# Adapter table rows stored unsplit, and split by GpSimd when a tile's rows are placed

## The reference, cut to what matters

```
x = x + x W^T + 2 * experts(x)        # W 1024x1024; 8 experts of rank 16, gated by the top 2
x = x + weights[cond] mixed over the 64 rows of a sample
x = x + (x B2[id]^T) A2[id]^T         # 64 adapters of rank 16, one for each sample
x = x + x W3^T + b3 + 2 * (x A3[m]) B3[m]   # 32 adapters of rank 16, one for each sample
```

## Time and profile before

| | us |
|---|---|
| median of three runs | 886.78 |
| span of the profiled execution | 884.5 |
| what lies around the span (median less span) | 2.3 |
| PE busy | 876.8 (99%) |
| DVE busy | 651.4 (74%) |
| ACT busy | 350.5 (40%) |
| POOL busy | 241.3 (27%) |
| granted PE clock, all 40 slices | 9 tenths or more |

### The profile page before, as it was taken

The page is one execution under the profiler, slowest core; times in us unless marked ns, Lnnn a source line. Parts: engine busy times, 40 slices in busy tenths (PEclk is TensorE's granted clock), DMA queues, the critical chain, the costliest instruction groups (busy, mean ns, idle before and its releaser), DMA issues.

```text
span 884.5 us, 15284 instructions
## 1 busy us (share of the span) xinstructions
PE 876.8 (99%) x4668; PEld 810.8 (92%) x4668; DVE 651.4 (74%) x1865; ACT 350.5 (40%) x800; POOL 241.3 (27%) x379
## 2 busy tenths in 40 slices
PE   8999999999999999999999999999999999999997
PEld 7888888888888889999999999999999999999997
DVE  6555444444358634798998899898899899899896
ACT  5544333333334423434434434434334344345333
POOL 1100010010000004415415425325325335235230
PEclk9999999999999999999999999999999999999999
DMA  7978686899663575566666667667667667566674
GB/s 243 311 265 282 207 262 211 284 350 274 191 193 126 162 222 174 164 179 200 213 185 216 202 182 230 196 188 222 192 188 230 185 195 224 186 195 215 196 205 144
DMA packets 105606, 187.71 MB, mean 212 GB/s; under 512 B 20022, under 2 KB 66870, under 8 KB 105526
## 3 DMA queue, kind: packets, MB, share of 16 engines
q1 hardware_dynamic: 105526, 186.76, 68.3%
HBM read 143.20 MB, written 49.81 MB: 218 GB/s over the span
## 4 chain that ended last, share of the span: by engine, by line
PE 96%; DMA 1%; DVE 1%; POOL 1%; SPq 0%; issue 0%; ACT 0%; DVEq 0%; POOLq 0%
PE ps_o L1487 28%; PE ps_w L1521 16%; PE ps_d L1513 15%; PE ps_d L1521 12%; PE ps_s L1487 9%; PE ps_o L1534 5%; PE ps_d L1528 4%; PE ps_o L1556 3%; PE ps_s L1562 1%; PE ps_w L1528 1%; DMA chunk_a_raw<-mov 1%; DMA stat_raw<-x 1%; PE ps_s L1568 0%; PE ps_o L1589 0%; DVE outb L1333 0%
## 5 line engine op out<-in xcount | busy, mean ns | idle before, releaser
L1094 DVE TENSOR_TENSOR stat_lo<-stat_raw,stat_hi 128x1024 fp32r<-128x1024 f32 (+1 forms) x127 | 152.2, 1199 | 22.2 <-ACT stat_hi L798 19.8
L798 ACT ACTIVATE stat_hi<-stat_raw 128x1024 fp32r<-128x1024 f32 (+1 forms) x127 | 116.7, 931 | 12.1 <-POOL stat_raw L682 5.4
L1513 PE MATMUL ps_d<-w_hi,stat_hi 128*128 128x392 f32 x256 | 86.9, 340 | 0.3 <-POOL w_lo L707 0.3
L1513 PE MATMUL ps_d<-w_hi,stat_lo 128*128 128x392 f32 x256 | 86.8, 339 | 0.0
L1513 PE MATMUL ps_d<-w_lo,stat_hi 128*128 128x392 f32 x256 | 86.8, 339 | 0.0
L1487 PE MATMUL ps_o<-chunk_a_hi,stat_hi 128*128 128x512 f32 x216 | 84.3, 390 | 0.9 <-DVE chunk_a_lo L1094 0.9
L1487 PE MATMUL ps_o<-chunk_a_lo,stat_hi 128*128 128x512 f32 x216 | 84.1, 389 | 0.0
L1487 PE MATMUL ps_o<-chunk_a_hi,stat_lo 128*128 128x512 f32 x216 | 84.0, 389 | 0.0
L707 POOL CAST w_hi<-mdraw 128x512 fp32r<-128x512 f32 x32 | 31.3, 977 | 157.0 <-DMA mdraw<-t 156.9
L682 POOL TENSOR_TENSOR stat_raw<-stat_raw,ident 128x128 f32<-128x128 f32 x40 | 20.5, 514 | 186.5 <-DMA stat_raw<-stat 186.5
L1487 PE MATMUL ps_o<-chunk_b_hi,stat_hi 128*128 128x512 f32 x152 | 59.1, 389 | 0.0
(11 more groups left out here) (230 smaller groups left out, 2346.4 us busy)
## 6 DMA issues: line engine op xcount, KB each, us to landing
up<-tu SPq DMA_DIRECT2D x124, 256.0 KB, 4.6
stat_raw<-stat SPq DMA_DIRECT2D x59, 512.0 KB, 4.2
mdraw<-t SPq DMA_DIRECT2D x128, 208.0 KB, 3.2
stat_raw<-x SPq DMA_DIRECT2D x32, 512.0 KB, 3.4
out<-outb SPq DMA_DIRECT2D x30, 512.0 KB, 5.5
t<-md_a SPq DMA_DIRECT2D x16, 576.0 KB, 5.4
rows_raw<-x SPq DMA_DIRECT2D x32, 256.0 KB, 3.7
chunk_a_raw<-mov SPq DMA_DIRECT2D x24, 256.0 KB, 5.5
```

The source lines that it names most:

```text
L798: return nc.scalar.activation(dst, src, ACT.Copy)
L1094: return nc.vector.tensor_tensor(out=dst, in0=src, in1=rounded.bitcast(F32), op=ALU.subtract)
L1513: last = nc.tensor.matmul(plain_bank(t)[:, 0:WCOLS], rows[a][:, k, :], w[c][:, k, :], start=k == 0 and m == 0, stop=k == KB - 1 and m == l ...
```

## The change

The tables hold the products in float32, one value for each instead of two parts. ACT's evacuation of the 27 groups of `D_CHUNKS` writes float32 (the same number of operations, of the same size), DVE's for these groups is gone, and PE, SP and the counts of `dve_ev` follow from that. A stored row is 144 + 128 = 272 columns instead of 416. Each of the three chunks has a buffer of its own. `place_w` and `place_b` now make the rounded part with a `tensor_copy` from float32 to float32r, wait for it, and make the rest with a `tensor_tensor` subtraction that reads `mdraw` and the part just written. `pool_md` and `pool_mb` count two for each tile. `mdraw` shrinks by 2304 bytes in each partition, and everything allocated behind it moves down by that.

```diff
-    RAW_AT, FULL = 2 * ROW, 2 * ROW + KB * RANK
+    RAW_AT, FULL = ROW, ROW + KB * RANK
...
+    def split_out(g):
+        return sum(GROUPS[n][0] in M3_CHUNKS for n in range(g + 1))
...
-            md_a = stages.enter_context(nc.sbuf_tensor("md_a", [P, PER, 2 * ROW], F32R))
-            md_b = stages.enter_context(nc.sbuf_tensor("md_b", [P, PER, 2 * ROW], F32R))
-        mdst = [md_a, md_b, md_a]
+            mdst = [stages.enter_context(nc.sbuf_tensor(f"md_{c}", [P, PER, ROW], F32)) for c in D_CHUNKS]
...
-        mdraw = sb("mdraw", [P, 2 * BT, FULL], F32R)
+        with nc.sbuf_tensor("up3_last", [P, D], F32R) as up3_b:
+            pass
+        mdraw = sb("mdraw", [P, 2 * BT, FULL])
...
             def store_md(c, n):
                 if n == 0:
-                    sp.wait_ge(dve_ev, LAST[c] + 1)
+                    sp.wait_ge(act_ev, LAST[c] + 1)
...
             def load_md(t):
                 if not at(t, 0):
-                    sp.wait_ge(pool_mb, t)
+                    sp.wait_ge(pool_mb, 2 * t)
...
             def place_w(t):
...
-                for part in (hi, lo):
-                    rows = mdraw[:, :, part * ROW:part * ROW + KB * RANK]
-                    last = nc.gpsimd.tensor_copy(w[part][:, :, MD_AT:P_AT].rearrange("p k (q r) -> p k q r", r=RANK),
-                                                 rows.rearrange("p q (k r) -> p k q r", r=RANK))
-                last.then_inc(pool_md, 1)
+                rows = mdraw[:, :, 0:KB * RANK].rearrange("p q (k r) -> p k q r", r=RANK)
+                upper_w, lower_w = [v[:, :, MD_AT:P_AT].rearrange("p k (q r) -> p k q r", r=RANK) for v in w]
+                nc.gpsimd.tensor_copy(upper_w, rows).then_inc(pool_md, 1)
+                pool.wait_ge(pool_md, 2 * t + 1)
+                nc.gpsimd.tensor_tensor(out=lower_w, in0=rows, in1=upper_w.bitcast(F32), op=ALU.subtract).then_inc(pool_md, 1)
...
             def place_b(t):
...
+                nc.gpsimd.tensor_copy(upper_b, rows).then_inc(pool_mb, 1)
+                pool.wait_ge(pool_mb, 2 * t + 1)
+                nc.gpsimd.tensor_tensor(out=lower_b, in0=rows, in1=upper_b.bitcast(F32), op=ALU.subtract).then_inc(pool_mb, 1)
...
-                    if c == 2 and g == FIRST[2]:
-                        act.wait_ge(st_md[0], 16 * STORES)
...
             def group_lo(g):
                 c, s = GROUPS[g]
+                if c in D_CHUNKS:
+                    return
...
-                if c in D_CHUNKS:
-                    rest(mdst[c][:, :, ROW + s * RANK:ROW + (s + 1) * RANK], src.rearrange("p (a r) -> p a r", r=RANK),
-                         mdst[c][:, :, s * RANK:(s + 1) * RANK]).then_inc(dve_ev, 1)
...
                 if g >= BANKS:
-                    pe.wait_ge(dve_ev, g - BANKS + 1)
+                    if GROUPS[g - BANKS][0] in D_CHUNKS:
+                        pe.wait_ge(act_ev, g - BANKS + 1)
+                    else:
+                        pe.wait_ge(dve_ev, split_out(g - BANKS))
...
-                pe.wait_ge(pool_md, a + 1)
+                pe.wait_ge(pool_md, 2 * a + 2)
```

More of the change, by code:

```diff
@@ L147, in build @@
     PAIRS = TILES // 2
-    t2 = nc.dram_tensor("t2", (NE2, P, FULL), F32R, kind="Internal").ap()
-    t3 = nc.dram_tensor("t3", (NE3, P, FULL), F32R, kind="Internal").ap()
+    t2 = nc.dram_tensor("t2", (NE2, P, FULL), F32, kind="Internal").ap()
+    t3 = nc.dram_tensor("t3", (NE3, P, FULL), F32, kind="Internal").ap()
     tu2 = nc.dram_tensor("tu2", (NE2, RANK, 2, D), F32R, kind="Internal").ap()
@@ L185, in build @@
         assert (kept_bytes + gap_bytes) % (8 * EVEN) == 0
-        assert 0 <= gap_bytes and 2 * PER * 2 * ROW * 4 <= kept_bytes + gap_bytes
+        assert 0 <= gap_bytes and len(D_CHUNKS) * PER * ROW * 4 <= kept_bytes + gap_bytes
         with ExitStack() as chunks:
@@ L333, in build @@
         FROM_PE = TILES - 3
-        up2_b, up3_b = [v[:, :, :].rearrange("p k t -> p (k t)")[:, 0:D] for v in (x0[hi], mdraw)]
+        up2_b = x0[hi][:, :, :].rearrange("p k t -> p (k t)")
         outb_b = x0raw[:, :, :].rearrange("p k t -> p (k t)")
@@ L433, in store_u2 @@
                 c, s = GROUPS[g]
-                sp.wait_ge(dve_ev, g + 1)
+                sp.wait_ge(dve_ev, split_out(g))
                 store_rows(tu2, tu_unit(g), s - U2_BLOCKS[0], SEGMENTS[c])
@@ L438, in store_md @@
                 if n == 0:
-                    sp.wait_ge(dve_ev, LAST[c] + 1)
+                    sp.wait_ge(act_ev, LAST[c] + 1)
                 table, first = (t2, c * PER) if c < 2 else (t3, 0)
                 own = slice(n * PER // STORES, (n + 1) * PER // STORES)
-                sp.dma_start(table[first + own.start:first + own.stop, :, 0:RAW_AT].rearrange("a p f -> p a f").bitcast(F32),
-                             mdst[c][:, own, :].bitcast(F32)).then_inc(st_md[c], 16)
+                sp.dma_start(table[first + own.start:first + own.stop, :, 0:RAW_AT].rearrange("a p f -> p a f"),
+                             mdst[c][:, own, :]).then_inc(st_md[c], 16)
             def store_own(n):
@@ L447, in store_own @@
                 table, source, first = (t2, u2k, first) if first < NE2 else (t3, d3k, first - NE2)
-                sp.dma_start(table[first:first + OWN, :, RAW_AT:FULL].bitcast(F32),
+                sp.dma_start(table[first:first + OWN, :, RAW_AT:FULL],
                              source[first:first + OWN].rearrange("a p k r -> a p (k r)")).then_inc(st_own, 16)
@@ L480, in load_md @@
                 if not at(t, 0):
-                    sp.wait_ge(pool_mb, t)
+                    sp.wait_ge(pool_mb, 2 * t)
                     sp.wait_ge(pool_ud, 2 * t)
                 for b in range(BT):
-                    sp.dma_start(mdraw[:, b, :].bitcast(F32), t2[chosen2[t][b]].bitcast(F32)).then_inc(ld_md, 16)
+                    sp.dma_start(mdraw[:, b, :], t2[chosen2[t][b]]).then_inc(ld_md, 16)
                 for b in range(BT):
-                    sp.dma_start(mdraw[:, BT + b, :].bitcast(F32), t3[chosen3[t][b]].bitcast(F32)).then_inc(ld_md, 16)
+                    sp.dma_start(mdraw[:, BT + b, :], t3[chosen3[t][b]]).then_inc(ld_md, 16)
             def load_mix(t, turn):
@@ L640, in last @@
                 load_mix(a, TURN_A)
-                sp.wait_ge(pool_md, TILES)
-                sp.wait_ge(pool_mb, TILES)
+                sp.wait_ge(pool_md, 2 * TILES)
+                sp.wait_ge(pool_mb, 2 * TILES)
                 sp.wait_ge(pool_ud, 2 * TILES)
@@ L713, in place_b @@
                     pool.wait_ge(pe_xp, t)
[L714 to L717, removed]
+                rows = mdraw[:, :, KB * RANK:ROW]
+                upper_b, lower_b = [v[:, 0:MD].rearrange("p (q r) -> p q r", r=RANK) for v in b03]
+                nc.gpsimd.tensor_copy(upper_b, rows).then_inc(pool_mb, 1)
+                pool.wait_ge(pool_mb, 2 * t + 1)
+                nc.gpsimd.tensor_tensor(out=lower_b, in0=rows, in1=upper_b.bitcast(F32), op=ALU.subtract).then_inc(pool_mb, 1)
             def ud_lo(t):
                 for n, (first, dst) in enumerate(((0, u2s), (BT, d3m))):
-                    raw = mdraw[:, first:first + BT, RAW_AT:FULL].bitcast(F32).rearrange("p b (k r) -> p b k r", r=RANK)
+                    raw = mdraw[:, first:first + BT, RAW_AT:FULL].rearrange("p b (k r) -> p b k r", r=RANK)
                     pool.wait_ge(act_ud, 2 * t + n + 1)
@@ L1109, in group_lo @@
                 c, s = GROUPS[g]
+                if c in D_CHUNKS:
+                    return
                 dve.wait_ge(act_ev, g + 1)
                 src = ps_g[g % BANKS][:, :]
[L1112 to L1115 removed]
+                if s in U2_BLOCKS:
                     q = tu_unit(g)
@@ L1141, in group_lo @@
                                                 op=ALU.subtract).then_inc(dve_ev, 1)
-                        dve.wait_ge(dve_ev, g + 1)
+                        dve.wait_ge(dve_ev, split_out(g))
                         nc.vector.tensor_tensor(out=T4raw[:, n, :], in0=B21[hi][:, n, :].bitcast(F32), in1=T2raw[:, n, :],
@@ L1603, in fore @@
                 pe.wait_ge(dve_x0, j + 1)
-                pe.wait_ge(pool_md, a + 1)
+                pe.wait_ge(pool_md, 2 * a + 2)
                 if at(j, 0):
                     pe.wait_ge(dve_hl, 1)
-                    pe.wait_ge(dve_ev, M_DONE + 1)
+                    pe.wait_ge(dve_ev, split_out(M_DONE))
                     pe.wait_ge(dve_set, SETS)
@@ L1616, in fore @@
                 if at(j, 0):
-                    pe.wait_ge(dve_ev, G)
+                    pe.wait_ge(dve_ev, split_out(G - 1))
                 hidden_product(a)
@@ L1630, in fore @@
                 pe.wait_ge(dve_x1, j + 1)
-                pe.wait_ge(pool_md, b + 1)
+                pe.wait_ge(pool_md, 2 * b + 2)
                 if not at(j, 0):
@@ L1645, in fore @@
                 pe.wait_ge(dve_hgT, a + 1)
-                pe.wait_ge(pool_mb, a + 1)
+                pe.wait_ge(pool_mb, 2 * a + 2)
                 experts(a, plain_bank(a)[:, HL:WCOLS], YP).then_inc(pe_xp, 1)
```

(2 more changed lines are left out.)

## The result

| | before | after |
|---|---|---|
| median, us | 886.57 (four runs) | 891.67 (890.9 to 893.85, four runs) |
| ratio to before | | 1.006 (95% interval 1.0046 to 1.0074) |
| span of the profiled execution | 884.5 | 890.9 |

The forecast was 887.1 with a range up to 891.5, so the median lies 0.2 us above the range. The profiled execution is the slowest of the four, 893.85 us; it shows 6.4 us of the difference, of which the median holds 5.1. The page's busy times are the first view.

The account below looks back on a forecast made before the run. PE sets the time, with DVE second at P6. Pair 0 at +0.2 and pairs with little to spare at +0.1 gave +0.3 us, span 884.5 to 884.8; with 2.3 us around it 887.1, range 885.4 to 891.5.

Parts of the forecast that it names:

- First part at 0: 9.2 to 340 us: removing 27 DVE subtractions (18.6 us) gains 0, because PE never waits there.
- later loads at 0: The 124 other loads of mdraw get a third shorter; nothing on PE waits for them: 0.
- second site at 0: Between 564 and 568 us place_w(a+2) can hold DVE by 0.1 to 0.9 us; DVE then waits anyway: 0.
- POOL's cover behind place_w(a+2): POOL's 1.18 us wait for PE there, all but used up by 1.1 us more work for a tile.
- POOL's own time: Second part: copies become subtractions with self-waits, 1.1 us for a tile, 36 us over 32 tiles.
- Pair 0 at +0.2: Subtraction ends 0.89 us later, a shorter load gives back 0.7: net +0.2 us, bounds -0.3 to +0.9.
- The race: POOL's w_lo subtraction against DVE's L1304 in each pair: DVE asks 0.05 us sooner and wins; +0.1 us in all.
- can start at 544.26: Pair 6: POOL's subtraction starts 0.14 us after w_hi ends at 544.12, behind DVE's request at 544.21.
- 0 us in nearly every pair: DVE gains 0.33 us at L1304 and gives it back at gdiff, leaving nothing for P6.
- rival 1: Race lost: POOL's subtraction goes before L1304, P6 pays 0.6 us in some 14 pairs, 8.5 us, 895.3; chance 0.13.
- "Operations that read two SBUF operands" exclude each other: POOL and DVE operations reading two SBUF operands exclude each other; the later one waits for the whole instruction.
- rival 3: Faster: DVE keeps 0.3 us, waits of pairs 0, 1 and 12 go, 885.9 us; chance 0.15 together with another rival.

Follow-up runs that it names:

- e2: The changed kernel with place_w's subtraction replaced by a plain copy without a wait: 885.89 us, ratio 0.9992 to the kernel before.
- e8: The kernel before with place_w's second copy replaced by the wait and subtraction, and DVE's L1304 made to go first in every pair: 892.88 us, ratio 1.0062.
- e5: The changed kernel with DVE's hidden_sum rewritten so each of its four operations reads one PSUM and one SBUF operand: 886.07 us, ratio 0.9991.
- e3: The changed kernel where, for odd tiles, POOL's subtraction also waits for DVE's L1304, so DVE always goes first: 886.75 us, ratio 0.9999.
- e4: The changed kernel where DVE's L1304 of pairs 1 to 15 waits for POOL's subtraction of the odd tile to finish: 904.74 us, ratio 1.0198.

## Why the prediction was wrong, step by step

- *First part at 0, later loads at 0, second site at 0:* right, by e2 and the windows. POOL's cover behind place_w(a+2) was called all but used up, with the shorter loads giving back about as much. They give back more: POOL waits 2.46 us for PE there ahead of pair 6, where it waited 1.25. How much hung on it shows in e8, where the rows are long and `ranks3` waits 5.0 us.
- *POOL's own time:* the subtraction was taken at 1.30 us and took 1305 ns, the small one 0.32 and took 349 ns; POOL grew by 34 us, not 36. That this is so near is partly luck: the sum counted the self-waits as busy time, which the profile doesn't, and left out that DVE holds the rounded copy for longer, 1127 ns in the mean instead of 977. The self-wait behind a copy was taken at 0.14 us and is 0.08.
- *Pair 0 at +0.2:* the sums came 0.67 us sooner (0.7 was counted) and the subtraction ended at 349.65 us against 349.49, +0.16. PE was 0.23 us later there for what came before, and its wait shrank from 0.30 to 0.23 us.
- *The race, "can start at 544.26", and with it "0 us in nearly every pair": this step failed.* It cost 0.5 us in twelve of fifteen pairs. The wait of a POOL instruction for its own predecessor was read as 0.14 us from a row with a subtraction ahead of it. The changed kernel has that pair of instructions too, and there it is 0.15 (541.97 + 1.31 = 543.28 to 543.43). Behind the rounded copy it is 0.07 by the rows (546.67 to 546.74), 0.08 when read in nanoseconds. The prediction had written down that the case turns at 0.09, that its margin was 0.05, and that its 0.14 did not come from behind a copy; with this figure POOL is up to 0.01 us ahead of DVE instead of 0.05 behind. Why the wait is shorter behind a copy stays open. Given that, the rest of rival 1 holds: gdiff gives nothing back, P6 pays. Its 0.6 us for a pair were 0.5, its 14 pairs were 12 and 10, since so close a race is won now and then; 8.5 us forecast for it, 5.1 measured.
- *"Operations that read two SBUF operands" exclude each other:* too narrow. It is DVE's operation that needs two; POOL's copies read one and still held L1304 for 0.33 us, and were held by x1_lo.
- *Chances:* rival 1 was given 0.13 on one row's figure. A step whose sign hangs on 0.05 us, in every pair alike, with the distance taken from another kind of instruction, was worth no more than an even chance, and the range should have held 895.
- *Faster, rival 3:* the best it could give was put at 885.9; e2 (885.89, without the subtraction) and e5 (886.07) are there, still within what can't be told from no change.

## What to carry to other kernels

Where two engines exclude each other instruction by instruction, lengthening one instruction can cost nothing on its own engine and still cost the other one: look for the other engine's short operations that ask at the same time, and ask what waits for them. If the order is decided by hundredths of a microsecond, don't predict it; fix it, by a semaphore that lets the short one go first (e3) or by taking away its second SBUF operand (e5). Look also for what ties the two engines together: here one long DVE instruction released both, so the near tie came back in every pair. An edit that shortens transfers can be paying silently for one that lengthens an engine's chain (e3 against e8), so test the two apart.

## What the runs showed of the hardware that was not expected

- A GpSimd instruction that waits for its own predecessor starts 0.08 us after a copy ends (64 cases, 512 and 64 columns), but 0.14 us after a `tensor_tensor` ends (16 cases), in the trace of the changed kernel; by rows of two decimals the distances come out as 0.07 and 0.15 too.
- A start in the record isn't yet who goes first: DVE's L1306 won three times although its record starts 2 to 5 ns behind that of POOL's subtraction.
- A DVE operation on two SBUF operands holds up a GpSimd copy that reads only one: 1.61 us instead of 0.61 under x1_lo.
- An instruction that waits on a semaphore for the other engine's instruction loses the shared operands to the next one in that engine's queue: DVE's request comes 0.10 us after the subtraction's end and takes 0.64 us instead of 0.18 (e4, 15 of 15 pairs). One that is already asking when the instruction ends gets in first.
